# A gated cross-attention kernel: the gated product written back into the PSUM bank of the context columns

## What is computed

```python
memory_proj = jnp.einsum('bme,de->bmd', memory, W_mem)
scores = jnp.einsum('bnd,bmd->bnm', hidden_states, memory_proj) / jnp.sqrt(jnp.float32(D))
attn = jax.nn.softmax(scores, axis=-1)
memory_context = jnp.einsum('bnm,bmd->bnd', attn, memory_proj)
gate_input = jnp.concatenate([hidden_states, memory_context], axis=-1)
gate = jax.nn.sigmoid(jnp.einsum('bnf,df->bnd', gate_input, W_gate) + b_gate)
fused = hidden_states + gate * memory_context
return _rmsnorm(fused, norm_w)
```

## Time and profile before

| | |
|---|---|
| median of 3 runs | 301.8 us (301.78 to 302.87) |
| the profiled execution's own time | 303.07 us |
| its span, from the first to the last instruction | 301.2 us |
| mean granted clock of PE | 0.994 of full speed |
| busy: PE, PEld | 288.2 us (96%), 249.6 us (83%) |
| busy: DVE, ACT, POOL | 190.1, 172.2, 160.4 us (63%, 57%, 53%) |
| DMA | 50.84 MB, mean 169 GB/s |

### The profile page before, as it was taken

The page is one execution under the profiler, slowest core; times in us unless marked ns, Lnnn a source line. Parts: engine busy times, 40 slices in busy tenths (PEclk is TensorE's granted clock), DMA queues, the critical chain, the costliest instruction groups (busy, mean ns, idle before and its releaser), DMA issues.

```text
span 301.2 us, 4992 instructions
## 1 busy us (share of the span) xinstructions
PE 288.2 (96%) x1638; PEld 249.6 (83%) x1638; DVE 190.1 (63%) x327; ACT 172.2 (57%) x364; POOL 160.4 (53%) x132
## 2 busy tenths in 40 slices
PE   6699999999999999999999999999999999999992
PEld 3599778878899988888889998888889998888881
DVE  3678367777674347787676236778766236877755
ACT  4768555656736555647736555765744755555442
POOL 0000645857944545685971844485991853555402
PEclk9999999999999999999999999999999999999997
DMA  6996733737572550857653352674744243543001
GB/s 206 405 361 216 255 121 109 232 117 246 169 239 76 171 202 18 255 176 227 208 182 131 103 178 98 195 238 148 243 146 173 96 148 103 155 148 119 35 37 70
DMA packets 20611, 50.84 MB, mean 169 GB/s; under 512 B 2288, under 2 KB 2544, under 8 KB 20592
## 3 DMA queue, kind: packets, MB, share of 16 engines
q1 hardware_dynamic: 20592, 50.60, 50.4%
HBM read 43.25 MB, written 7.34 MB: 168 GB/s over the span
## 4 chain that ended last, share of the span: by engine, by line
PE 86%; DVE 5%; ACT 4%; DMA 2%; issue 1%; SPq 1%; DVEq 0%; POOL 0%; POOLq 0%
PE gate_ps L294 34%; PE ctx_ps L294 14%; PE am_bank L294 12%; PE q_ps L294 12%; PE score_ps L294 11%; PE pT_ps L334 3%; DMA work<-in_wgT 2%; DVE work L700 2%; PE am_bank L351 2%; DVE top L666 1%; ACT work L532 1%; DVE pT_lo L654 1%; ACT pT_hi L500 1%; ACT mem_hi L500 0%; ACT probs L525 0%
## 5 line engine op out<-in xcount | busy, mean ns | idle before, releaser
L837 POOL TENSOR_TENSOR memT_lo<-memT_raw,memT_hi 128x752 fp32r<-128x752 f32 x30 | 55.8, 1860 | 82.9 <-ACT memT_hi L500 82.9
L837 POOL TENSOR_TENSOR mem_lo<-mem_raw,mem_hi 128x768 fp32r<-128x768 f32 x30 | 55.4, 1847 | 2.7 <-ACT mem_hi L500 2.3
L294 PE MATMUL gate_ps<-wgx_hi,xT_hi 128*128 128x512 f32 x112 | 44.6, 398 | 0.0
L294 PE MATMUL gate_ps<-wgx_hi,xT_lo 128*128 128x512 f32 x112 | 43.9, 392 | 0.0
L294 PE MATMUL gate_ps<-wgx_lo,xT_hi 128*128 128x512 f32 x112 | 43.8, 391 | 0.0
L625 ACT ACTIVATE am<-am_bank,share 112x256 f32<-112x256 f32 x32 | 15.2, 474 | 47.8 <-PE am_bank L294 47.8
L700 DVE SCALAR_TENSOR_TENSOR work<-work,x_rows 128x512 f32<-128x512 f32 (+1 forms) x29 | 41.6, 1436 | 0.6
L654 DVE TENSOR_TENSOR pT_lo<-pT_ps,pT_hi 128x336 fp32r<-128x336 f32 x32 | 16.2, 507 | 36.0 <-ACT pT_hi L500 36.0
L708 DVE SCALAR_TENSOR_TENSOR work<-work,rstd,norm_w 128x512 f32<-128x512 f32 (+1 forms) x29 | 35.3, 1220 | 1.0 <-POOL rstd L898 1.0
L525 ACT ACTIVATE probs<-score_ps,shift 112x375 f32<-112x375 f32 x32 | 18.4, 574 | 25.1 <-DVE shift L668 25.1
L855 POOL TENSOR_TENSOR guarded<-meansq,eps 128x1 f32<-128x1 f32 x27 | 5.1, 190 | 47.3 <-ACT work L532 47.3
(11 more groups left out here) (101 smaller groups left out, 727.5 us busy)
## 6 DMA issues: line engine op xcount, KB each, us to landing
mem_raw<-in_mem SPq DMA_DIRECT2D x32, 384.0 KB, 3.9
memT_raw<-in_memT SPq DMA_DIRECT2D x32, 376.0 KB, 3.0
x_rows<-in_x SPq DMA_DIRECT2D x28, 256.0 KB, 4.3
out<-work SPq DMA_DIRECT2D x27, 256.0 KB, 4.6
xT_raw<-in_xT SPq DMA_DIRECT2D x8, 640.0 KB, 6.6
xT_raw<-in_xT SPq DMA_DIRECT2D x3, 512.0 KB, 5.0
work<-in_wgT SPq DMA_DIRECT2D x2, 512.0 KB, 8.6
x_rows<-in_wgT SPq DMA_DIRECT2D x2, 512.0 KB, 10.7
```

The lines of the kernel that those rows point to most:

```text
L294: mm = pe.matmul(out, left, right, start=first and i == 0, stop=last and i == n - 1)
L837: return pool.tensor_tensor(out, in_, high.bitcast(F32), ALU.subtract)
```

## The change

`gate_context` writes its product over the context columns, in the bank `ctx_ps`, instead of into a slice of `work`, and `fuse` reads it there. The bank is thus in use until `fuse` is done, and `context` waits for `h_ready` (raised by `fuse`) where it waited for `u_ready`. The last two tiles of the last group keep u in SBUF (`late_u`), as before. The count, the kinds and the order of the instructions are the same on each engine.

```diff
-        u, squares = work[:, 6], work[:, 7]
+        late_u, squares = work[:, 6], work[:, 7]
...
-            def context(g, t, part=WHOLE, cols=ALL, bank=ctx_ps):
+            def context(g, t, part=WHOLE, cols=ALL, bank=ctx_ps, late=False):
                 pe.wait_ge(wmT_lo_ready, EC)
                 if t > 0 and part[0] == 0:
 
-                    pe.wait_ge(u_ready, TILES * g + t)
+                    pe.wait_ge(u_ready if late else h_ready, TILES * g + t)
...
-                        context(g, TILES - 1, cols=cols, bank=bank)
+                        context(g, TILES - 1, cols=cols, bank=bank, late=True)
...
-            def gate_context(g, t, cols=ALL, i=0, bank=ctx_ps):
+            def gate_context(g, t, cols=ALL, i=0, bank=ctx_ps, u=ctx_ps):
 
                 dve.wait_ge(tanh_ready, TILES * g + t + 1 + i)
                 dve.wait_ge(ctx_done, TILES * g + t + 1 + i)
                 dve.scalar_tensor_tensor(out=u[:, cols], in0=z[:, t % 2, cols], scalar=1.0, in1=bank[:, cols],
                                          op0=ALU.add, op1=ALU.mult).then_inc(u_ready, 1)
 
-            def fuse(g, t, cols=ALL, i=0):
+            def fuse(g, t, cols=ALL, i=0, u=ctx_ps):
...
                 amT_low(g, GROUP - 1)
-                gate_context(g, TILES - 2)
-                fuse(g, TILES - 2)
                 if last:
+                    gate_context(g, TILES - 2, u=late_u)
+                    fuse(g, TILES - 2, u=late_u)
                     for cols in HALVES:
                         add_bias(g, TILES - 1, cols)
                     for i, cols in enumerate(HALVES):
-                        gate_context(g, TILES - 1, cols, i, late_ps[i])
+                        gate_context(g, TILES - 1, cols, i, late_ps[i], late_u)
                     for i, cols in enumerate(HALVES):
-                        fuse(g, TILES - 1, cols, i)
+                        fuse(g, TILES - 1, cols, i, late_u)
...
                 else:
+                    gate_context(g, TILES - 2)
+                    fuse(g, TILES - 2)
                     q_low(g + 1, 0, 0)
```

## The result

The changed kernel takes 300.85 us (median of 8 runs, 300.4 to 302.58), the kernel before 303.14 us (8 runs, 301.78 to 304.49, the three known ahead of the prediction among them). The ratio is 0.994, with a 95% interval of 0.9912 to 0.9969. By the ratio it is faster by about 0.6%, some 1.8 us; the two medians lie 2.3 us apart, and the interval allows 0.9 to 2.7 us. The profiled execution took 301.01 us, with a span of 299.2.

A forecast was written before the change was run, and what follows sets the result against it. PE, busy 96%, was taken as the bound, so only its waits hanging on fuse could pay. Stalls of 1.55 and 0.22 us gave -1.77 us; from the median, 301.8 - 1.8 = 300.0 us, range 299.5 to 301.8.

The forecast's parts named there:

- Part 1: On DVE, fuse in all but two tiles takes 0.69 us; DVE busy time falls about 22 us, nearly all worth nothing.
- the rival: The missed gap: in blocks 4, 6 and 7 of three groups, an earlier mem_lo delays norm; 309 us, chance 0.04.
- Parts 2 and 3: PE's stalls at attend vanish: block 5 of groups 0 to 2, 1.55 us; block 3 of groups 1 to 3, 0.22 us.
- Part 4: gate_context writing PSUM takes 0.69 us; at a bound of 1.25 us, some 17 blocks lose 0 to 1.7 us.
- Part 5: Bank held until fuse ends: free in blocks, 0.46 us in time at group ends; uncovered, 0.29 us three times.
- Part 6: fuse's PSUM source: 65 ns dearer by the skill page, 1.75 us over 27 instructions; nil by the profile rows.
- The lock: fuse stays held by POOL as long as either input is in SBUF: 302.7 us, chance 0.05.
- The missed gap: Blocks 4, 6, 7, three groups: mem_lo ends before norm issues, xT_lo holds norm about 3 us; 309 us, chance 0.04.

The follow-up runs named there:

- the run that makes `norm` miss its gap: Changed kernel plus a second DVE instruction in front of add_bias in all whole tiles, output into an unused SBUF tile: 306.64 us, ratio 1.0128 to the kernel before.
- the run with the extra product: Changed kernel plus a second DVE instruction before each gate_context that writes PSUM, output into unused SBUF: 302.15 us, ratio 0.9986 to the kernel before.
- the longer hold alone: Kernel before with u kept in SBUF, but context waiting for h_ready instead of u_ready: 303.42 us, ratio 1.0038 to the kernel before.

## Why the prediction was right

**What bounds the kernel.** Right. 30 us less DVE time gave 2 us, and what can be located (1.73 us) is in the places where PE waited for `pT_lo` or where it came a little late.

**Part 1, fuse at 0.69 us.** Right, 0.690. The fall of DVE's busy time was put at 22 us and was 30. What I left out is `norm`, whose own busy time fell from 34.4 to 24.3 us: once `square` comes earlier, so does `mem_lo`, and `norm`, which is held until `mem_lo` ends, is held for less. Group 1, block 7 of the changed kernel, to compare with the earlier trace rows, timeline of POOL and DVE:

```profile
148.26 1.85 POOL L839 TENSOR_TENSOR mem_lo<-mem_raw,mem_hi 128x768 fp32r<-128x768 f32 x1
...
149.63 1.03 DVE L708 SCALAR_TENSOR_TENSOR work<-work,rstd,norm_w 128x512 f32<-128x512 f32 x1
```

I had worked out the shift of `mem_lo` for the rival, and did not apply it to the sum. It was off the path, so it cost the forecast nothing.

**Parts 2 and 3, the sum.** The three stalls of block 5 went from 1.78, 1.82 and 1.82 to 1.29, 1.30 and 1.29 us: 1.54 us against 1.55. Block 3 of groups 1 to 3 went from 1.37, 1.35 and 1.37 to 1.30 each: 0.19 against 0.22. `pT_hi` was to start 0.49 us behind the transposes and does. Together 1.73 of the 1.77 us; the middle as a whole shrank by 1.63, 1.77 and 1.52 us in the three executions.

**Part 4, the PSUM output.** 0.694 us against 0.69. My bound for a dear one had about the right size (1.32 us inside 0 to 1.7) and the wrong place.

**Part 5, the hold.** Cover of 0.46 us predicted, 0.45 found. The price without the cover was put at 0.29 us a time and measured at 0.38: the missing term is the 0.08 to 0.11 us that the second matmul behind a wait is late.

**Part 6, the price of a PSUM source.** The 65 ns that the prediction worked out, as an estimate, from the Trainium skill, "VectorE: DVE Perf Modes", section on the TRN2 errata, do not show: `fuse` took 0.68 to 0.69 undisturbed with its source in SBUF, and 0.690 with it in PSUM.

**The rivals.** The lock did not stay: of the 26 `fuse` with u in PSUM none is over 0.69 us. The missed gap did not occur: `mem_lo` ended at 150.11, 0.48 us behind the start of `norm`, where I had given some 0.45. Forced, it cost 5.65 us over the changed kernel; the prediction's sum has 9.0 there (309 us is 9 above its 300.0), with nine misses at 1.0 where there were six at about 0.9.

**The number.** 300.0 was forecast and 300.85 measured, inside the range. The difference of 1.8 us was right (0.6% by the ratio, with an interval of 0.9 to 2.7 us). The base was not: the median before was 301.8 by three runs and 303.14 by eight. The profiled execution, at 303.07, was nearer to it than I took it to be. So the absolute number rests on a base that was 1.3 us too low, and that it fell inside the range shows less than the difference and the places do.

**What stays open.** Why the start of one and the same kernel differs from run to run, below, is not shown. And every hold here is behind one form of POOL instruction, a subtraction of fp32 tensors, and met by DVE instructions with two fp32 tensors; other forms were not tried.

## What to carry to other kernels

Where DVE and POOL both stream SBUF, look at the length of each DVE form by where its operands are: the instruction whose time depends on what POOL does is the one with two SBUF inputs, and keeping one of them in a PSUM bank that is free anyway makes its time its own. Such a change pays only at the places where the tensor engine waits behind that instruction, so count those stalls one by one, and take the instructions' own saving for nothing, unless it frees such a place. And before moving work in another engine's order instead, follow what the moved step triggers: here as much time was lost again, in another wait, at the group's end.

## What the runs showed of the hardware

POOL and DVE hold each other, by whole instructions. A DVE instruction of 128x512 with two SBUF inputs that meets a running subtraction of POOL ends about 0.55 us behind POOL's end, whatever POOL's length (0.99, 1.81 or 2.94 us). POOL waits in its turn: `xT_lo` reads 2.94 us where it goes first (144.49, in the run that makes `norm` miss its gap) and 3.42 us where a `norm` queued ahead of it goes first (152.09 in the earlier trace rows), and a `memT_lo` queued behind a held `fuse` reads 2.27 to 2.29 us instead of 1.81. In these places the one that had been queued first went next. Coming 0.14 us behind the end of `mem_lo` cost `norm` 2.6 us.

A DVE instruction that reads and writes the same PSUM bank in place costs the same as one that writes SBUF, 0.694 us, against 0.686 us in the kernel before. Behind a wait of PE the second matmul comes 0.07 to 0.11 us later than it otherwise would, on top of the wait itself.

The kernel's start varies. In the windows of two executions of the same changed kernel (columns: us of the stretch, busy time of PE, PEld, DVE, ACT and POOL with their counts, granted clock, DMA share, GB/s), the first is the one compared in the result, the second a repeat:

```profile
11.00:16.00 5.00, 4.80 (x25) 4.34 (x26) 4.37 (x10) 3.53 (x7) 0.00 (x0) 1.00 1.03 420
```

```profile
11.00:16.00 5.00, 4.91 (x15) 4.04 (x16) 3.53 (x6) 3.41 (x7) 0.00 (x0) 0.66 1.03 419
```

In the second the granted clock averages 0.66: from 12.3 to 15.3 a matmul of 512 columns takes 0.43 us to the next instead of 0.23, the step of the lower level, 1.2 GHz. PE had stood idle for 2.06 us before 11.09 there, waiting for `wgc_lo`, but for 2.3 us in the run with the extra product too, where the clock stayed at 2.4 GHz. The first `attend` comes 1.45 us later (24.45 against 23.00). This is as much as these two executions differ (302.32 and 301.01 us). It is not the whole of the spread: in traces whose clock stayed at 1.00 in this window, the first `attend` comes anywhere from 21.02 (the longer hold alone) to 23.38 (the kernel before). In the three sets of runs the executions of the kernel before that took over 304 us have a mean granted clock of 0.988 to 0.993, those under 303.2 us one of 0.993 to 0.999; their starts were not traced. The difference between the kernels is another matter: the middle shows it without the start.
